# Seven of the sixteen units of a group by 32x32 block transposes and HBM instead of six, in an attention + MoE kernel on Trainium2

## The chip, the cores and the metric

One core of one Trainium2 chip. The time is the device time of one execution in microseconds (us). The kernel before takes 242.75 us (median of 3 runs, 242.49 to 242.84).

## What is computed

Two samples of 512 tokens with 128 channels. The part that fills most of the time, and the only one that the change touches, is attention with a convolution of the scores along the keys:

```python
Q, K, V = (query @ W.T + b, split in 16 heads of 8)
scores  = Q @ K.T / sqrt(8)                     # per head 512 x 512
scores  = conv1d over keys, 3 taps, per head     # H -> H, kernel size 3
weights = softmax(scores)
out     = weights @ V, heads joined, @ Wo.T + bo
```

(The convolution mixes the 16 heads; the kernel folds it into a key tensor of its own for every output head.) Ahead of it stands a gated MLP with one of eight experts for each sample, behind it a low-rank projection and a routed feed-forward layer of eight experts.

## The kernel before, in words

**Units and groups.** Attention is cut into 128 units: 2 samples x 16 heads x 4 tiles of 128 queries. A group is 4 heads, 16 units (u = 0 to 15), and there are 8 groups. A group has two pairs of heads: w = 0 is units 0 to 7, w = 1 is units 8 to 15. For each unit:

- TensorE makes the scores (128 queries x 512 keys) with three matmuls (L855 to L857), four units ahead of the rest, into one of four PSUM banks.
- VectorE takes the row minimum of the negated scores and copies them to SBUF (`maximum`, L592), also four units ahead.
- ScalarE takes the exponential in place (`exp`, L398).
- The weights must be turned so that keys lie on partitions. There are two ways. **By PE**: four transposes on TensorE (L995), and ScalarE copies the PSUM bank to SBUF (L442). **By blocks**: VectorE transposes 32x32 blocks (L719) into a staging tile `TB`, and once for each pair of heads the SP queue writes `TB` to a buffer `swap` in HBM (L218) and reads it back with the blocks in their places into `PTB` (four DMAs, L223).

**Which unit goes which way** is written out by hand: `by_blocks` (L181) takes the units with u % 8 in (0, 3, 5), six of sixteen. The last pair of the last group (`last_pair`) goes by PE alone. `by_pe` and `nth_blocks` number the units of the two ways for the semaphores `eva` (PE ways copied out) and `tb` (block transposes done).

**The crossing.** `cross(pair, w, gi)` (L214) on SP waits for the pair's last block transpose (`tb`), issues the write, waits for its landing (`ts`), issues the four reads (landing counted in `tm`). SP does nothing else in this stretch. For w = 0 the last block transpose is that of unit 5, for w = 1 that of unit 13.

**The outputs.** `outputs(pair, w, gi)` (L861) on TensorE multiplies the turned weights of a pair of heads with the values, once both ways have delivered: it waits for `eva` and for `tm`. It stands at the end of unit 15 for w = 0, and at the end of unit 7 *of the next group* for w = 1. TensorE works strictly in order, so the scores of unit 12 of that next group, issued at its unit 8, stand behind the outputs of w = 1. Four column tiles of 32 (two heads x two halves of each) are used side by side; three of the four have matmuls 256 wide, and the odd head of the half that mixes both ways has twice as many of 128 (L881), since its tiles lie in two buffers, `PTB` and `PTC`. After the outputs of w = 1 VectorE copies the bank out (`raw_out`, L599, at its unit 8) and goes on with its `maximum` of unit 12.

**Order on VectorE.** In unit u: extra work of the unit (`raw_out` at 8, `normalise` at 9, in the second sample parts of the next stages by `AT_DVE`), the maximum of unit u + 4, the block transpose of unit u if it goes by blocks, and at u % 4 = 2 the middle tap of a later head's keys (L536).

Of the kernel before, what the change touches and what calls it, by code (L numbers as in the profile page):

```python
# [19 lines left out]
B, S, C = 2, 512, 128  # L20
# [43 lines left out]
def build(nc, cond, wexp, xT, wqkvo, lora, cols, b2row, w1, w2, consts, out, swap):  # L64
# [4 lines left out]
    with ExitStack() as ctx:  # L69
# [75 lines left out]
        D = sb("D", [128, NT, T], f32r)  # L145

        flat = PT[:, :]
        half, cross_words = 8 * S, 4 * QT * 96
        PTA = flat[:, 0:half].rearrange("p (g k c) -> p g k c", g=G, k=QT)
        PTB = flat[:, half:half + 2 * cross_words].rearrange("p (w i k c) -> p w i k c", w=2, k=QT, i=4)  # L150
        PTC = flat[:, half + 2 * cross_words:16 * S].rearrange("p (w k c) -> p w k c", w=2, k=QT)
        staging = w2s[:, :, :, :].rearrange("p e j c -> p (e j c)")
        TB = staging[:, 0:2 * cross_words].rearrange("p (w i k c) -> p w i k c", w=2, k=QT, i=4)
        PTX = staging[:, cross_words:cross_words + 2048].rearrange("p (h k c) -> p h k c", h=2, k=QT)
        Ub = [[flat[:, (4 * b + i) * 512:(4 * b + i + 1) * 512] for i in range(2)] for b in range(B)]
        Tb = [[flat[:, (4 * b + 2 + i) * 512:(4 * b + 3 + i) * 512] for i in range(2)] for b in range(B)]
        Sb_ = [[flat[:, 4096 + (4 * b + i) * 512:4096 + (4 * b + i + 1) * 512] for i in range(2)] for b in range(B)]
# [21 lines left out]
            return b == B - 1 and isinstance(g, int) and g == NG - 1 and u >= U // 2  # L179

        def by_blocks(b, g, u):  # L181
            return u % 8 in (0, 3, 5) and not last_pair(b, g, u)

        def tile_of(b, g, u):
            return u % QT if last_pair(b, g, u) else TILE[u % 8]
# [1 line left out]
        def by_pe(b, g, u):  # L187


            at = u % 8 // 2 if last_pair(b, g, u) else (None, 0, 1, None, 2, None, 3, 4)[u % 8]  # L190
            return 10 * (NG * b + g) + 5 * (u // 8) + at

        def nth_blocks(b, g, u):
            return 6 * (NG * b + g) + 3 * (u // 8) + (0, 3, 5).index(u % 8)


        @block.sync
        def _(sp):
            sp.dma_start(condS[:, :], cond).then_inc(s["cond"], 16)
            sp.dma_start(xTs[:, 0:S], xT[:, 0:S]).then_inc(s["xt0"], 16)  # L200
            sp.wait_ge(s["cidx"], B)
            for b in range(B):
                e = sp.value_load(cidx[0:1, 8 * b:8 * b + 1], min_val=0, max_val=E - 1)
                for part, at, end in (("up", 0, WGT), ("down", WGT, EW)):
                    sp.dma_start(we[:, b:b + 1, at:end], wexp[bass.ds(e, 1), :, at:end]
                                 .rearrange("e p n -> p e n")).then_inc(s[f"{part}{b}"], 16)
                if b == 0:
                    sp.dma_start(xTs[:, S:T], xT[:, S:T]).then_inc(s["xt1"], 16)
            sp.dma_start(cst[:, :], consts).then_inc(s["cst"], 16)
            sp.dma_start(w1s[:, :, :], w1).then_inc(s["w1"], 16)  # L210
            sp.dma_start(b2s[:, :], b2row).then_inc(s["b2"], 16)
            sp.dma_start(out[T:2 * T, :].rearrange("(p a) c -> p (a c)", p=128), xT).then_inc(s["dump"], 16)

            def cross(pair, w, gi):  # L214

                sp.wait_ge(s["tb"], 3 * pair + 3)
                sp.wait_ge(s["pv"], pair)
                sp.dma_start(swap[:, w, :, :], TB[:, w, :, :, :].rearrange("p i k c -> p i (k c)"))\  # L218
                    .then_inc(s[f"ts{w}"], 16)
                sp.wait_ge(s[f"ts{w}"], 16 * gi + 16)  # L220
                by_source = swap.rearrange("(i p) w j n -> p w j i n", i=4)
                for j in range(4):
                    sp.dma_start(PTB[32 * j:32 * j + 32, w, :, :, :].rearrange("p i k c -> p i (k c)"),  # L223
                                 by_source[:, w, j, :, :]).then_inc(s[f"tm{w}"], 16)

            with sp.Fori(0, B * NG - 1) as g:
                for w in range(2):
                    cross(2 * g + w, w, g)
            cross(2 * (B * NG - 1), 0, B * NG - 1)
            sp.wait_ge(s["pv"], 4 * NG + 2)  # L230
            sp.dma_start(w2s[:, :, :, :], w2).then_inc(s["w2"], 16)
            rows = out[0:T, :].rearrange("(t p) c -> p t c", p=128)
            for b in range(B):
                sp.wait_ge(s["xte"], b + 1)
                sp.dma_start(rows[:, QT * b:QT * (b + 1), :], X1[:, QT * b:QT * (b + 1), :]).then_inc(s["outd"], 16)
            sp.wait_ge(s["outd"], 16 * B)
            sp.wait_ge(s["dump"], 16)
            sp.wait_ge(s["add"], 16 * E)
# [105 lines left out]
        def _(act):  # L344
# [83 lines left out]
            def unit(b, g, u):  # L428

                n = U * (NG * b + g) + u  # L430
                hd = H * b + G * g + u // QT
                if b == 1 and isinstance(g, int) and (g, u) in AT_ACT:
                    after(0, AT_ACT[g, u])
                if u % 2 == 1 if last_pair(b, g, u) else not by_blocks(b, g, u):

                    nth = by_pe(b, g, u)
                    bank = TP[1 if last_pair(b, g, u) else by_pe(0, 0, u) % 2]
                    half_tile, parity = divmod(tile_of(b, g, u), 2)
                    dst = PTA[:, u // QT % G, :, half_tile * 128:(half_tile + 1) * 128] if parity else \
                        PTC[:, u // 8, :, :]  # L440
                    act.wait_ge(s["tp"], nth + 2)
                    act.activation(dst, bank[:, :].rearrange("p (k q) -> p k q", k=QT), ACT.Copy)\  # L442
                        .then_inc(s["eva"], 1)
                if not isinstance(g, int) or n + AHEAD < U * NG * B:
                    exp(n + AHEAD, (u + AHEAD) % RING)
                if u % QT == 3 and (not isinstance(g, int) or hd + 3 < B * H):
                    high_half(hd + 3, (u // QT + 1) % 2)
                if u == 9:
                    stage_values(b, g)
# [51 lines left out]
        def _(dve):  # L501
# [181 lines left out]
            def unit(b, g, u):  # L683
# [22 lines left out]
                if last_pair(b, g, u) and u % 2 == 0:  # L706
                    dve.wait_ge(s["tpx"], (u - U // 2) // 2 + 1)
                    if u == U // 2:
                        dve.wait_ge(s["ts1"], 16 * (B * NG - 1))
                    dve.tensor_copy(PTX[:, j % 2, :, half_tile * 128:(half_tile + 1) * 128],  # L710
                                    TP[0][:, :].rearrange("p (k q) -> p k q", k=QT))\
                        .then_inc(s["evx"], 1)
                elif by_blocks(b, g, u):

                    if u % (2 * QT) == 0 and (not isinstance(g, int) or b + g > 0):
                        dve.wait_ge(s[f"ts{w}"], 16 * (NG * b + g))
                    dve.wait_ge(s["ex"], n + 2)
                    at = 64 * (j % 2) + 32 * half_tile
                    dve.transpose(TB[:, w, :, :, at:at + 32].rearrange("p i k c -> p k i c"),  # L719
                                  Pb[:, u % RING, :].rearrange("p (k i c) -> p k i c", i=4, c=32)).then_inc(s["tb"], 1)  # L720
                if u % QT == 2 and (not isinstance(g, int) or H * b + G * g + j + 3 < B * H):
                    over = isinstance(g, int) and G * g + j + 3 >= H
# [72 lines left out]
        def _(pe):  # L795
# [63 lines left out]
            def outputs(pair, w, gi):  # L859


                pe.wait_ge(s["eva"], 5 * pair + 6)
                pe.wait_ge(s[f"tm{w}"], 64 * gi + 64)
                if w == 0:
                    pe.wait_ge(s["vst"], gi + 1)
# [1 line left out]
                for k in range(QT):  # L867
                    for f in range(2):
                        for i in range(2):
                            at = 32 * (2 * f + i)  # L870
                            bank, v = PV[at:at + VW, 256 * w:256 * w + 256], Vst[:, k, 2 * w + i, :]
                            ends = dict(start=(k == 0), stop=(k == QT - 1))
                            if f:
                                mm = pe.matmul(bank, v, PTA[:, 2 * w + i, k, :], **ends)  # L874
                            elif i == 0:
                                pe.matmul(bank, v, PTB[:, w, :, k, 0:64].rearrange("p i (t c) -> p t i c", t=2), **ends)  # L876
                            else:
                                t = k // 2
                                for kk in (2 * k % QT, 2 * k % QT + 1):
                                    x = PTC[:, w, kk, :] if t else PTB[:, w, :, kk, 64:96]  # L880
                                    pe.matmul(bank[:, 128 * t:128 * t + 128], Vst[:, kk, 2 * w + i, :], x,  # L881
                                              start=(kk == 0), stop=(kk == QT - 1))
                mm.then_inc(s["pv"], 1)

            def last_outputs(l):
# [1 line left out]

                bank = (PV[:, 256:384], SC[3][:, 0:128])[l]
                pe.wait_ge(s["evx"], 3 + l)
                pe.wait_ge(s["eva"], 10 * B * NG - 1 + l)  # L890
                for k in range(QT):
                    for f in range(2):
                        for i in range(2):
# [79 lines left out]
            def unit(b, g, u):  # L973
# [7 lines left out]
                if not by_blocks(b, g, u):  # L981
# [8 lines left out]
                    else:  # L990
                        bank = TP[by_pe(0, 0, u) % 2]
                        if not isinstance(g, int) or nth > 0:
                            pe.wait_ge(s["eva"], nth)
                    for k in range(QT):
                        mm = pe.transpose(bank[:, k * 128:(k + 1) * 128],  # L995
                                          Pb[:, u % RING, k * 128:(k + 1) * 128], ident)
# [178 lines left out]
```

## Time and profile before

| what | value |
|---|---|
| median of 3 runs | 242.75 us |
| the profiled execution | 245.08 us, of which the span is 243.0 us |
| TensorE (PE) busy | 225.3 us, 93% |
| VectorE (DVE) busy | 194.5 us, 80% |
| ScalarE (ACT) busy | 165.1 us, 68% |
| GpSimd (POOL) busy | 162.0 us, 67% |
| chain that ended last | PE 70%, DVE 10%, issue 8%, POOL 4%, ACT 3%, DMA 2% |

Groups run from about 30 us to 200 us of the span. A busy share is an average over stages; a PE that is busy all the time may still run at a lower granted clock (a separate column of the windows view). Start times in the timeline are from the span's start; matmuls overlap one another, so what one costs is the distance from its start to the next one's, not its own duration.

### The profile page before, as it was taken

What the parts mean: (1) busy time and instruction counts of PE and PEld (TensorE: products, weight loads), DVE (VectorE), ACT (ScalarE), POOL (GpSimd) and SP (SyncE); (2) the same over time, 40 slices, a digit from 0 to 9 for tenths busy, and PEclk for the clock granted to TensorE, in tenths of its full rate; (3) what the DMA queues carried; (4) which work ended last, traced back from release to release, by engine and by line L of the source; (5) the groups of instructions that cost most, each with busy time, mean ns of one, the idle gap of its engine ahead of it and who ended that gap; (6) DMA issues with size and microseconds to landing.
All of it is one profiled execution on the core that took longest, in us unless ns stands there. A gap on an engine that the chain in (4) does not pass through costs nothing.

```text
span 243.0 us, 5432 instructions
## 1 busy us (share of the span) xinstructions
PE 225.3 (93%) x1733; PEld 178.3 (73%) x1733; DVE 194.5 (80%) x485; ACT 165.1 (68%) x297; POOL 162.0 (67%) x190
## 2 busy tenths in 40 slices
PE   7897986799989999999999999999999989999980
PEld 7444764588868788878876876878788866688980
DVE  2548899979898998997998899989989783375470
ACT  2554577989788988989778569799798770212510
POOL 1008986889969989898886668889983600052785
PEclk9999799999999999999999999999999999999997
DMA  6990000745627454574535353636476440840233
GB/s 201 364 386 0 0 4 39 205 157 122 207 57 220 166 129 160 121 219 147 132 133 129 132 129 131 132 136 155 154 206 133 161 101 4 294 138 3 22 32 32
DMA packets 14933, 32.77 MB, mean 135 GB/s; under 512 B 1586, under 2 KB 11826, under 8 KB 14642
## 3 DMA queue, kind: packets, MB, share of 16 engines
q1 hardware_dynamic: 13330, 31.35, 42.9%
q0 software_dynamic: 1152, 0.52, 2.5%
q10 hardware_dynamic: 432, 0.65, 0.8%
q8 instruction: 11, 0.18, 0.3%
q14 instruction: 8, 0.07, 0.1%
HBM read 19.67 MB, written 13.37 MB: 136 GB/s over the span
## 4 chain that ended last, share of the span: by engine, by line
PE 70%; DVE 10%; issue 8%; POOL 4%; ACT 3%; DMA 2%; POOLq 1%; SPq 0%; DVEq 0%; ACTq 0%
PE tp L995 12%; PE sc L855 11%; PE sc L857 10%; PE sc L856 10%; PE pvbank L876 6%; PE pvbank L874 5%; POOL out L338 4%; DVE Pb L592 3%; PE sc L1047 2%; PE sc L817 2%; PE sc L1048 1%; DMA we<-in_wexp 1%; PE misc L902 1%; ACT Kh L393 1%; DVE kc L536 1%
## 5 line engine op out<-in xcount | busy, mean ns | idle before, releaser
L398 ACT ACTIVATE Pb<-Pb,nbias 128x512 f32<-128x512 f32 x128 | 90.6, 719 | 26.0 <-DVE Pb L592 24.8
L592 DVE TENSOR_SCALAR_CACHE_REDUCE Pb<-sc,col 128x512 f32<-128x512 f32 x128 | 91.8, 733 | 11.5 <-PE sc L857 10.2
L855 PE MATMUL sc<-Kh,Ql 128*128 128x512 f32 x124 | 57.0, 460 | 3.0 <-POOL Kl L262 1.4
L995 PE MATMUL tp<-cst,Pb 128*128 128x128 f32 x332 | 49.8, 273 | 3.2 <-ACT PT L442 2.3
L995 PEld LDWEIGHTS tp<-cst,Pb 128*128 128x128 f32 x332 | 40.5, 140 | 15.9 <-issue 4.2
L262 POOL TENSOR_TENSOR Kl<-kc,Kh 128x512 fp32r<-128x512 f32 x29 | 37.3, 1287 | 17.9 <-ACT Kh L393 16.7
L857 PE MATMUL sc<-Kh,Qh 128*128 128x512 f32 x124 | 48.9, 394 | 0.0
L856 PE MATMUL sc<-Kl,Qh 128*128 128x512 f32 x124 | 48.7, 393 | 0.0
L442 ACT ACTIVATE PT<-tp 128x512 f32<-128x512 f32 x79 | 45.9, 581 | 1.7 <-PE tp L995 1.2
L274 POOL TENSOR_TENSOR td<-ta,tc_ 128x512 f32<-128x512 f32 x31 | 44.4, 1431 | 2.6
L267 POOL TENSOR_SCALAR ta<-Kp,cwS 128x512 f32<-128x512 f32 x31 | 23.4, 755 | 16.0 <-ACT Kp L371 15.9
L719 DVE STREAM_TRANSPOSE w2s<-Pb 128x512 f32<-128x512 f32 x45 | 31.7, 704 | 0.0
L855 PEld LDWEIGHTS sc<-Kh,Ql 128*128 128x128 f32 x124 | 23.4, 189 | 9.6 <-issue 5.3
L536 DVE SCALAR_TENSOR_TENSOR kc<-Kp,col,td 128x512 f32<-128x512 f32 x31 | 29.5, 952 | 0.0
L874 PE MATMUL pvbank<-PT,Vst 128*32 128x256 f32 x240 | 29.3, 386 | 0.0
L881 PE MATMUL pvbank<-PT,Vst 128*32 128x128 f32 x240 | 29.0, 274 | 0.0
L876 PE MATMUL pvbank<-PT,Vst 128*32 128x256 f32 x120 | 28.7, 382 | 0.2 <-DMA PT<-swap 0.2
L269 POOL TENSOR_SCALAR tc_<-Kp,cwS 128x512 f32<-128x512 f32 x31 | 27.6, 889 | 0.0
L857 PEld LDWEIGHTS sc<-Kh,Qh 128*128 128x128 f32 x124 | 23.3, 188 | 5.5
L881 PEld LDWEIGHTS pvbank<-PT,Vst 128*32 128x32 f32 x240 | 25.0, 110 | 0.0
L856 PEld LDWEIGHTS sc<-Kl,Qh 128*128 128x128 f32 x124 | 23.6, 190 | 1.8 <-issue 0.2
L393 ACT ACTIVATE Kh<-kc 128x512 fp32r<-128x512 f32 x30 | 18.5, 617 | 0.9 <-DVE kc L536 0.9
(213 smaller groups left out, 289.4 us busy)
## 6 DMA issues: line engine op xcount, KB each, us to landing
swap<-w2s SPq DMA_DIRECT2D x15, 768.0 KB, 3.3
PT<-swap SPq DMA_DIRECT2D x60, 192.0 KB, 3.9
w1s<-in_w SPq DMA_DIRECT2D x1, 2048.0 KB, 9.7
w2s<-in_w SPq DMA_DIRECT2D x1, 2048.0 KB, 10.1
cst<-in_consts SPq DMA_DIRECT2D x1, 652.0 KB, 5.2
xTs<-in_xT SPq DMA_DIRECT2D x2, 256.0 KB, 3.3
we<-in_wexp SPq DMA_DIRECT2D x2, 256.0 KB, 3.6
b2s<-in_b2row SPq DMA_DIRECT2D x1, 512.0 KB, 10.4
```

Of the source, the lines that this page charges most:

```text
L262: pool.tensor_tensor(Kl[:, n, :], kc[:, n, :], Kh[:, n, :].bitcast(f32), ALU.subtract)\
L274: pool.tensor_tensor(td[:, n, :], ta[:, :], tc_[:, :], ALU.add).then_inc(s["d"], 1)
L398: act.activation(Pb[:, k, :], Pb[:, k, :], ACT.Exp, bias=nbias[:, k:k + 1], scale=-1.0)\
L442: act.activation(dst, bank[:, :].rearrange("p (k q) -> p k q", k=QT), ACT.Copy)\
L592: dve.tensor_scalar(Pb[:, k, :], SC[k % 4][:, :], cb, None, ALU.subtract, ALU.min, accum_out=nbias[:, k:k + 1]).then_inc(s["mx"], 1)
L855: pe.matmul(SC[k][:, :], ql, Kh[:, h2, :], start=True, stop=False)
L856: pe.matmul(SC[k][:, :], qh, Kl[:, h2, :], start=False, stop=False)
L857: pe.matmul(SC[k][:, :], qh, Kh[:, h2, :], start=False, stop=True).then_inc(s["sc"], 1)
L874: mm = pe.matmul(bank, v, PTA[:, 2 * w + i, k, :], **ends)
L876: pe.matmul(bank, v, PTB[:, w, :, k, 0:64].rearrange("p i (t c) -> p t i c", t=2), **ends)
L881: pe.matmul(bank[:, 128 * t:128 * t + 128], Vst[:, kk, 2 * w + i, :], x, start=(kk == 0), stop=(kk == QT - 1))
L995: mm = pe.transpose(bank[:, k * 128:(k + 1) * 128], Pb[:, u % RING, k * 128:(k + 1) * 128], ident)
```

## The change

`by_blocks` takes unit 15 too, so that seven units of a group go by blocks: units 0, 3, 5 for w = 0 and units 8, 11, 13, 15 for w = 1. Nine go by PE instead of ten. The numbers in the semaphore waits follow. `cross` for w = 1 waits for the transpose of unit 15 instead of unit 13, and moves four words of width 32 for every block column instead of three: 512 words for each row piece instead of 384. `swap` becomes one tensor with rows of 896 words, of which w = 0 has the first 384 and w = 1 the other 512, so a partition's four pieces no longer lie behind one another in HBM. In `outputs` the odd head of w = 1 now lies wholly in `PTB`, so its matmuls are 256 wide; the one of w = 0 stays as it was. TensorE's wait at unit 1 is for one more `eva`, since nine is odd and units 14 and 1 now use the same PSUM bank. Nothing changes in the last pair of the last group.

```diff
@@ -145,13 +145,15 @@
-        half, cross_words = 8 * S, 4 * QT * 96
+        half, cross_words = 8 * S, (4 * QT * 96, 4 * QT * 128)
...
@@ -179,7 +181,7 @@
         def by_blocks(b, g, u):
-            return u % 8 in (0, 3, 5) and not last_pair(b, g, u)
+            return (u % 8 in (0, 3, 5) or u == U - 1) and not last_pair(b, g, u)
@@ -188,10 +190,10 @@
-            return 10 * (NG * b + g) + 5 * (u // 8) + at
+            return 9 * (NG * b + g) + 5 * (u // 8) + at
 
         def nth_blocks(b, g, u):
-            return 6 * (NG * b + g) + 3 * (u // 8) + (0, 3, 5).index(u % 8)
+            return 7 * (NG * b + g) + 3 * (u // 8) + (0, 3, 5, 7).index(u % 8)
@@ -213,15 +215,15 @@
             def cross(pair, w, gi):
 
-                sp.wait_ge(s["tb"], 3 * pair + 3)
+                sp.wait_ge(s["tb"], 3 * pair + gi + (3 + w))
                 sp.wait_ge(s["pv"], pair)
-                sp.dma_start(swap[:, w, :, :], TB[:, w, :, :, :].rearrange("p i k c -> p i (k c)"))\
-                    .then_inc(s[f"ts{w}"], 16)
+                crossing = swap[:, :, 384 * w:384 + 512 * w]
+                sp.dma_start(crossing, TB[w].rearrange("p i k c -> p i (k c)")).then_inc(s[f"ts{w}"], 16)
                 sp.wait_ge(s[f"ts{w}"], 16 * gi + 16)
-                by_source = swap.rearrange("(i p) w j n -> p w j i n", i=4)
+                by_source = crossing.rearrange("(i p) j n -> p j i n", i=4)
                 for j in range(4):
-                    sp.dma_start(PTB[32 * j:32 * j + 32, w, :, :, :].rearrange("p i k c -> p i (k c)"),
-                                 by_source[:, w, j, :, :]).then_inc(s[f"tm{w}"], 16)
+                    sp.dma_start(PTB[w][32 * j:32 * j + 32, :, :, :].rearrange("p i k c -> p i (k c)"),
+                                 by_source[:, j, :, :]).then_inc(s[f"tm{w}"], 16)
@@ -861,7 +861,7 @@
             def outputs(pair, w, gi):
 
-                pe.wait_ge(s["eva"], 5 * pair + 6)
+                pe.wait_ge(s["eva"], 9 * gi + (6, 10)[w])
                 pe.wait_ge(s[f"tm{w}"], 64 * gi + 64)
@@ -873,11 +875,14 @@
+                            elif w:
+                                mm = pe.matmul(bank, v, PTB[w][:, :, k, 64:128].rearrange("p i (t c) -> p t i c", t=2),
+                                               **ends)
                             else:
                                 t = k // 2
                                 for kk in (2 * k % QT, 2 * k % QT + 1):
-                                    x = PTC[:, w, kk, :] if t else PTB[:, w, :, kk, 64:96]
+                                    x = PTC[:, kk, :] if t else PTB[w][:, :, kk, 64:96]
@@ -990,7 +995,7 @@
-                            pe.wait_ge(s["eva"], nth)
+                            pe.wait_ge(s["eva"], nth + 1 if u == 1 else nth)
@@ -1168,7 +1173,7 @@
-    swap = nc.dram_tensor("swap", (128, 2, 4, 384), mybir.dt.float32, kind="Internal").ap()
+    swap = nc.dram_tensor("swap", (128, 4, 896), mybir.dt.float32, kind="Internal").ap()
```

## Rows read from the trace of the kernel before

**Rows 1.** Costliest groups (busy, mean ns, idle before and its releaser): the outputs
```profile
L876 PE MATMUL pvbank<-PT,Vst 128*32 128x256 f32 x120 | 28.7, 382 | 0.2 <-DMA PT<-swap 0.2
```

**Rows 2.** Windows: us, busy of PE, PEld, DVE, ACT, POOL, PEclk, DMA
```profile
83.65:94.11 10.46, 10.46 (x92) 8.49 (x89) 9.99 (x27) 9.09 (x16) 9.22 (x11) 1.00 0.51 143
94.11:103.97 9.86, 9.86 (x88) 8.12 (x85) 8.84 (x22) 8.62 (x16) 8.86 (x10) 1.00 0.54 150
```

**Rows 3.** Timeline of PE: start, duration, line, operation; outputs, then units
```profile
102.03 0.40 PE L876 MATMUL pvbank<-PT,Vst 128*32 128x256 f32 x1
...
106.03 0.60 PE L995 MATMUL tp<-cst,Pb 128*128 128x128 f32 x4
...
107.16 0.60 PE L995 MATMUL tp<-cst,Pb 128*128 128x128 f32 x4
...
108.30 0.39 PE L855 MATMUL sc<-Kh,Ql 128*128 128x512 f32 x1
...
108.99 0.60 PE L995 MATMUL tp<-cst,Pb 128*128 128x128 f32 x4
```

**Rows 4.** Timeline of DVE at the end of a group (units 13 to 16)
```profile
91.42 0.70 DVE L719 STREAM_TRANSPOSE w2s<-Pb 128x512 f32<-128x512 f32 x1
92.05 0.70 DVE L592 TENSOR_SCALAR_CACHE_REDUCE Pb<-sc,col 128x512 f32<-128x512 f32 x1
...
93.41 0.74 DVE L592 TENSOR_SCALAR_CACHE_REDUCE Pb<-sc,col 128x512 f32<-128x512 f32 x1
...
95.18 0.75 DVE L592 TENSOR_SCALAR_CACHE_REDUCE Pb<-sc,col 128x512 f32<-128x512 f32 x1 [1.02 <-PE sc L857]
```

**Rows 5.** Timeline of SP, third group, w = 1: write and four reads issued
```profile
92.15 0.34 SPq L218 DMA_DIRECT2D swap<-w2s  x1
95.41 1.73 SPq L223 DMA_DIRECT2D PT<-swap  x4
```

**Rows 6.** DMA view of single issues: slowest write; first and last reads of a crossing
```profile
swap<-w2s SPq DMA_DIRECT2D x1, 768.0 KB, 5.4
...
PT<-swap SPq DMA_DIRECT2D x1, 192.0 KB, 2.9
...
PT<-swap SPq DMA_DIRECT2D x1, 192.0 KB, 4.3
```

**Rows 7.** Chain that ended last: the load of 16 numbers (64 bytes)
```profile
0.73 1.20 DMA condS<-in_cond
```

**Rows 8.** Timeline of SP: w = 1 writes of groups 0, 3 and 4
```profile
49.77 0.34 SPq L218 DMA_DIRECT2D swap<-w2s  x1
...
112.21 0.34 SPq L218 DMA_DIRECT2D swap<-w2s  x1
...
135.64 0.34 SPq L218 DMA_DIRECT2D swap<-w2s  x1
```

**Rows 9.** Timeline of PE: the outputs that those writes lead to
```profile
60.42 0.40 PE L876 MATMUL pvbank<-PT,Vst 128*32 128x256 f32 x1
...
123.25 0.40 PE L876 MATMUL pvbank<-PT,Vst 128*32 128x256 f32 x1
...
148.51 0.40 PE L876 MATMUL pvbank<-PT,Vst 128*32 128x256 f32 x1
```

**Rows 10.** Timeline of DVE in group 4: maxima of units 18 and 20
```profile
135.53 0.71 DVE L592 TENSOR_SCALAR_CACHE_REDUCE Pb<-sc,col 128x512 f32<-128x512 f32 x1
...
140.56 0.75 DVE L592 TENSOR_SCALAR_CACHE_REDUCE Pb<-sc,col 128x512 f32<-128x512 f32 x1
```

**Rows 11.** Windows ahead of the first groups (columns as in rows 2)
```profile
22.50:24.70 2.20, 0.02 (x2) 0.05 (x1) 2.11 (x4) 1.20 (x2) 2.10 (x3) 1.00 0.00 0
...
25.00:26.00 1.00, 1.00 (x5) 0.77 (x3) 1.00 (x2) 0.33 (x1) 0.92 (x2) 0.65 0.00 0
26.00:28.00 2.00, 2.00 (x6) 1.63 (x5) 1.66 (x5) 1.13 (x3) 1.86 (x3) 0.50 0.00 0
28.00:29.00 1.00, 1.00 (x4) 0.77 (x4) 0.62 (x1) 0.61 (x1) 1.00 (x2) 0.65 0.00 0
```

More of the change, by code:

```diff
@@ L147, in build @@
         flat = PT[:, :]
-        half, cross_words = 8 * S, 4 * QT * 96
+        half, cross_words = 8 * S, (4 * QT * 96, 4 * QT * 128)
         PTA = flat[:, 0:half].rearrange("p (g k c) -> p g k c", g=G, k=QT)
-        PTB = flat[:, half:half + 2 * cross_words].rearrange("p (w i k c) -> p w i k c", w=2, k=QT, i=4)
-        PTC = flat[:, half + 2 * cross_words:16 * S].rearrange("p (w k c) -> p w k c", w=2, k=QT)
+        PTB = [a.rearrange("p (i k c) -> p i k c", k=QT, i=4) for a in
+               (flat[:, half:half + cross_words[0]], flat[:, half + cross_words[0]:half + sum(cross_words)])]
+        PTC = flat[:, half + sum(cross_words):16 * S].rearrange("p (k c) -> p k c", k=QT)
         staging = w2s[:, :, :, :].rearrange("p e j c -> p (e j c)")
-        TB = staging[:, 0:2 * cross_words].rearrange("p (w i k c) -> p w i k c", w=2, k=QT, i=4)
-        PTX = staging[:, cross_words:cross_words + 2048].rearrange("p (h k c) -> p h k c", h=2, k=QT)
+        TB = [a.rearrange("p (i k c) -> p i k c", k=QT, i=4) for a in
+              (staging[:, 0:cross_words[0]], staging[:, cross_words[0]:sum(cross_words)])]
+        PTX = staging[:, cross_words[0]:sum(cross_words)].rearrange("p (h k c) -> p h k c", h=2, k=QT)
         Ub = [[flat[:, (4 * b + i) * 512:(4 * b + i + 1) * 512] for i in range(2)] for b in range(B)]
@@ L439, in unit @@
                     dst = PTA[:, u // QT % G, :, half_tile * 128:(half_tile + 1) * 128] if parity else \
-                        PTC[:, u // 8, :, :]
+                        PTC[:, :, :]
                     act.wait_ge(s["tp"], nth + 2)
@@ L718, in unit @@
                     at = 64 * (j % 2) + 32 * half_tile
-                    dve.transpose(TB[:, w, :, :, at:at + 32].rearrange("p i k c -> p k i c"),
+                    dve.transpose(TB[w][:, :, :, at:at + 32].rearrange("p i k c -> p k i c"),
                                   Pb[:, u % RING, :].rearrange("p (k i c) -> p k i c", i=4, c=32)).then_inc(s["tb"], 1)
@@ L875, in outputs @@
                             elif i == 0:
-                                pe.matmul(bank, v, PTB[:, w, :, k, 0:64].rearrange("p i (t c) -> p t i c", t=2), **ends)
+                                pe.matmul(bank, v, PTB[w][:, :, k, 0:64].rearrange("p i (t c) -> p t i c", t=2), **ends)
+                            elif w:
+                                mm = pe.matmul(bank, v, PTB[w][:, :, k, 64:128].rearrange("p i (t c) -> p t i c", t=2),
+                                               **ends)
                             else:
@@ L889, in last_outputs @@
                 pe.wait_ge(s["evx"], 3 + l)
-                pe.wait_ge(s["eva"], 10 * B * NG - 1 + l)
+                pe.wait_ge(s["eva"], 9 * B * NG + l)
                 for k in range(QT):
```

## The prediction

> **What bounds the kernel now.** First the windows, to see which engine has no gap. In a settled group of 20.32 us PE is busy in all of it at the full granted clock, 10.46 us for the half with units 8 to 15 and 9.86 us for the other; DVE is busy for 9.99 and 8.84 us, ACT for less, POOL for 9.22 and 8.86 us [rows 2]. So a settled group costs what PE's queue costs, and DVE has 1.5 us to spare in it. Then the costliest groups, for what PE waits for ahead of the outputs: DMA made it wait 0.2 us in the whole execution [rows 1]. The crossings through HBM are hidden. The question that these two views leave open is by how much, since the change makes a crossing both later and larger; the timelines of SP and PE answer it.
>
> **What it removes.** From transpose to transpose a unit that goes by PE takes 107.16 - 106.03 = 1.13 us of PE, a unit by blocks 108.99 - 108.30 = 0.69 us [rows 3], so unit 15 frees 0.44 us. It does so in seven groups (not in the last): 3.1 us, which is the whole gain if nothing else moves. The odd head's matmuls go from eight of 128 columns to four of 256. The columns are the same, and the other three column tiles stream 256 of them at the same time, so I take nothing for it; between 0 and 0.1 us a group of issuing may go. ACT has one copy less in each, and it is not the bound.
>
> **What it adds on DVE.** A block transpose takes 92.05 - 91.42 = 0.63 us. It stands behind the maximum of unit 19. There DVE ran out of work: that maximum starts at 93.41, would be done by 94.15, and the next starts at 95.18 after 1.02 us of waiting for scores [rows 4]. The transpose fits in this gap even when PE comes 0.44 us sooner. If the cover were gone it would cost 0.63 us a group. TensorE's changed wait at unit 1 is for a copy made two units earlier; nothing for it. On SP the next crossing (w = 0) waits for a transpose of unit 5, some 7 us later, while issuing the larger one holds SP 4.0 + 1.8 us, so SP is free again; that write may queue behind the reads of the larger crossing, but its own outputs are then later too.
>
> **What it moves: the start of the crossing of w = 1.** Before, the write is issued at 92.15, right behind the transpose of unit 13 (91.42 + 0.63) [rows 4, 5]. Now the wait is for unit 15's. Between the two DVE has the maximum of 18, a middle tap, the maximum of 19 (93.41 - 92.05 = 1.36 us to its start, 0.67 us for itself by the same spacing as its neighbours) and the transpose, 0.63 us: **2.65 us later**.
>
> **And its length.** Before, the write of 768 KB lands in 95.41 - 92.15 = 3.26 us [rows 5]. Now it is 1 MB. The nearest rows bound what the third more costs: nothing, if the time is not in the bytes (3.3 us), or in proportion (4.35 us). With 1.2 us of it fixed, as in the load of 64 bytes [rows 7], it is 1.2 + 2.06 x 4/3 = **4.0 us**, which I take; the writes have also taken up to 5.4 us [rows 6]. Of the four reads, issued over 1.73 us (0.43 apart), the first lands after 2.9 us and the fourth 1.30 + 4.3 = 5.6 us after the first issue [rows 5, 6], so three more reads of 192 KB cost 2.7 us, 0.9 us each, twice their issue spacing: they queue for bandwidth. With 256 KB I take 1.2 us each and 3.2 us for the first, **6.8 us**; the ends are 5.6 us (the count of pieces sets the time, and it is the same) and 7.5 us (all in proportion). With 0.06 us between landing and first read [rows 5] and 0.1 us for PE to start, a crossing from the end of the transpose to the outputs is 0.1 + 4.0 + 0.06 + 6.8 + 0.1 = 11.1 us.
>
> The Trainium skill, "DMA: Bandwidth & Descriptors" (section on the two cost components), gives a DMA about 2.0 us fixed and 436 GB/s beyond. By it the write of 1 MB would take 4.4 us, 0.4 us more than taken above, but 3.8 us for the old one, where the trace has 3.26; the measurement decides.
>
> **How much room there was.** From the issue of the write to the outputs: third group 102.03 - 92.15 = 9.88 us [rows 3, 5], and groups 1, 5 and 6 lie within 0.25 us of it (four in all, taken at 9.85); group 0 60.42 - 49.77 = 10.65; group 3 123.25 - 112.21 = 11.04; group 4 148.51 - 135.64 = 12.87 [rows 8, 9]. New need, counted from the old issue: 2.65 + 4.0 + 0.06 + 6.8 + 0.1 = 13.61 us. In group 4 DVE has the gate work between the two transposes: from 135.53 to 140.56 and a transpose of 0.63 [rows 10], 5.66 us in place of 2.65, so 16.6 us. PE then stands still at the end of unit 7 for longer than before: 3.0 us (group 0), 4 x 3.76 = 15.0, 2.6 (group 3), 3.75 (group 4): **24.4 us**. Is any of it got back? Behind the outputs PE has scores 12, and DVE its copy of the bank and every maximum up to 19, then the next trigger; that way from outputs to trigger was DVE's without a gap already, so the lost time is lost in every turn. And PE's 0.44 us is not on this loop at all: it only makes PE wait earlier. So the 3.1 us are **not** subtracted.
>
> **The clock.** PE stood still from 22.5 to 24.7 us ahead of the first groups, and the granted clock then fell from full (2.4 GHz) to half (1.2 GHz) over about 3.4 us: 0.65, 0.50, 0.50, 0.65 in the microseconds from 25 to 29 [rows 11]. The new stalls, the wait above plus the freed 0.44 us, are of 3 to 4.2 us, longer than that one. If each is followed by such a stretch, up to 1.7 us of PE's work is lost in it, and part of the stretch lies in the stall itself. Between 0 and 1.7 us I take 0.9 us, seven times: **6.3 us**.
>
> The Trainium skill, "TensorE: Matmul & The Clock Gate" (section "HAM oscillation"), describes the same: PE waiting for a DMA in each turn goes back to half rate each time. The row agrees so far that one idle stretch did it; no row shows whether it repeats.
>
> **Sum.** Against the profiled execution: 245.08 + 24.4 + 6.3 = 275.8 us. That execution is 2.3 us above the median of the runs, 242.75; the added terms are the same for both, so I predict **273.5 us** for the median.
>
> **Rivals.**
> - *Stalls without the clock.* PE does 20 us of work between stalls, and small gaps elsewhere left the clock full [rows 2]. For it: only one stretch in the trace shows a fall. Then 242.75 + 24.4 = 267.2 us, between 261 and 273 with the bounds on the transfers.
> - *Size costs nothing*, only the later start does (3.3 and 5.6 us). Each stall is 1.9 us shorter: 24.4 - 13.3 = 11.1, 253.9 us. Against it: the reads queue at 0.9 us each. Stalls of under 2 us would hardly touch the clock.
> - *The other side, faster.* The crossing stays hidden, and PE's 0.44 us count: 242.75 - 3.1 = 239.65 us. It decides at a crossing of 9.88 - 2.65 - 0.44 = 6.8 us from trigger to outputs; the present one, smaller, already takes 3.26 + 5.6 = 8.9 us. I see nothing in the trace that would shorten it.
> - *The change does nothing measurable*, because gains and stalls cancel (0.44 us a stall). Every settled group would have to stall that little.
>
> **Chances.** Stalls and half clock 0.50 (own range 265 to 284); stalls, full clock 0.33; size free 0.12; faster 0.03; no difference 0.02. A difference of 0.2%, about what a measurement of this kernel can tell, is 0.5 us, and no case but the last lies in it. The range goes from 256 (between size-free and full clock) to 283 (half clock with slower transfers: the writes at 4.35, the reads at 7.5 us would add 1.05 x 7 = 7.4 us).
>
> **What would show it.** PE idle ahead of the first outputs matmul of w = 1 (L876), released by the DMA into PT, about 3 to 4 us long and seven times; the write of w = 1 issued right behind the transpose of unit 15, landing in 4.0 us; the last read 6.8 us after the first issue; the group's period near 24 us in place of 20.3; DVE and ACT with idle time in the same place; seven dips in the granted clock right behind the stalls. It is wrong if L876's idle is under 10 us in sum, if the write is issued sooner than 2 us behind unit 13's transpose, or if the clock stays full.

## The result, and the profile after

The changed kernel takes **285.25 us** (median of 4 runs, 284.34 to 288.94) against 242.8 us: a ratio of 1.171, with a 95% interval of 1.165 to 1.177. It is 42.5 us slower, 2.3 us above the upper end of the range and 11.8 us above the forecast of 273.5 us. The execution whose trace is shown took 288.94 us, with a span of 286.9 us and a mean granted clock of 0.906; the other three took 284.3 to 286.1 us at 0.920 to 0.923, and the ratio is that of these three fast runs alone, which is why it lies below 285.25 / 242.8 = 1.175.

The page of the profile, busy time, granted clock in 40 slices, and the chain that ended last:

```profile
PE 239.8 (84%) x1649; PEld 178.5 (62%) x1649; DVE 197.8 (69%) x492; ACT 161.8 (56%) x290; POOL 159.0 (55%) x190
...
PEclk9997999986997799689959997899699959999998
...
PE 36%; DMA 26%; DVE 19%; issue 9%; SPq 3%; POOL 3%; ACT 1%; POOLq 1%; DVEq 0%
DMA PT<-swap 14%; DMA swap<-w2s 11%; DVE Pb L594 9%; PE pvbank L878 8%; PE sc L857 4%; DVE w2s L721 4%; POOL out L340 3%; PE tp L1000 3%; PE sc L859 3%; PE sc L858 3%; SPq L225 3%; DVE kc L538 2%; PE sc L1052 1%; PE sc L819 1%; PE sc L1053 1%
```

PE has fallen from 93% to 84% of a longer span, and DMA has gone from 2% to 26% of the chain. Each crossing of w = 1 stands in it now, both its halves.

The costliest groups, with the idle time before them and what ended it. What was 0.2 us in [rows 1] is now 29.9 us (28.8 us of it ahead of the seven outputs of w = 1, 1.0 us ahead of the first outputs of w = 0), and the copy behind the outputs (L601) waits as well:

```profile
L878 PE MATMUL pvbank<-PT,Vst 128*32 128x256 f32 x120 | 40.4, 498 | 29.9 <-DMA PT<-swap 29.9
L601 DVE COPY RAW<-pvbank 128x512 f32<-128x512 f32 x7 | 4.8, 692 | 41.9 <-PE pvbank L876 41.9
```

Timeline of PE, one turn of the loop: outputs of w = 1 and the scores behind them, then the next outputs of w = 1:

```profile
91.49 0.60 PE L878 MATMUL pvbank<-PT,Vst 128*32 128x256 f32 x1 [4.62 <-DMA PT<-swap]
...
95.06 0.80 PE L857 MATMUL sc<-Kh,Ql 128*128 128x512 f32 x1
...
118.76 0.61 PE L878 MATMUL pvbank<-PT,Vst 128*32 128x256 f32 x1 [4.87 <-DMA PT<-swap]
```

A period, from one set of outputs of w = 1 to the next, is 27.3 us instead of 20.3. The outputs take 3.57 us from their start to the next scores, where they took 83.61 - 81.71 = 1.90 us, though the odd head's are fewer. The kernel before, PE and then DVE (the maximum of unit 12), in the same turn:

```profile
81.71 0.40 PE L876 MATMUL pvbank<-PT,Vst 128*32 128x256 f32 x1
...
83.61 0.50 PE L855 MATMUL sc<-Kh,Ql 128*128 128x512 f32 x1
...
84.76 0.75 DVE L592 TENSOR_SCALAR_CACHE_REDUCE Pb<-sc,col 128x512 f32<-128x512 f32 x1 [0.32 <-PE sc L857]
```

The seven stalls on the DMA are 3.34, 4.62, 4.87, 3.69, 2.96, 4.78 and 4.58 us long.

Timeline of DVE in the same turn, the copy of the bank, the maximum of unit 12, then the maximum of unit 19, the transpose of unit 15, and the first step of the next group:

```profile
95.19 0.69 DVE L601 COPY RAW<-pvbank 128x512 f32<-128x512 f32 x1 [6.15 <-PE pvbank L876]
96.89 0.75 DVE L594 TENSOR_SCALAR_CACHE_REDUCE Pb<-sc,col 128x512 f32<-128x512 f32 x1 [1.01 <-PE sc L859]
...
105.66 0.74 DVE L594 TENSOR_SCALAR_CACHE_REDUCE Pb<-sc,col 128x512 f32<-128x512 f32 x1
...
106.33 0.70 DVE L721 STREAM_TRANSPOSE w2s<-Pb 128x512 f32<-128x512 f32 x1
106.96 0.70 DVE L594 TENSOR_SCALAR_CACHE_REDUCE Pb<-sc,col 128x512 f32<-128x512 f32 x1
```

Timeline of SP: the crossing of w = 1 that this transpose releases, then that of w = 0:

```profile
107.06 0.52 SPq L221 DMA_DIRECT2D swap<-w2s  x1
111.47 1.73 SPq L225 DMA_DIRECT2D PT<-swap  x4
113.76 0.52 SPq L221 DMA_DIRECT2D swap<-w2s  x1
120.28 1.73 SPq L225 DMA_DIRECT2D PT<-swap  x4
```

The write goes out 0.10 us behind unit 15's transpose (106.33 + 0.63, the spacing to the next step) and lands in 4.4 us; from the first read to the outputs it is 118.76 - 111.47 = 7.29 us. The fourth read is issued at 112.77 and takes 5.9 us:

```profile
PT<-swap SPq DMA_DIRECT2D x1, 256.0 KB, 5.9
```

It lands at 118.67, and PE starts 0.1 us behind it. That makes 11.7 us from the write's issue to the outputs (11.5 to 11.7 us in all seven). The write of w = 0 queues behind the reads and takes 6.5 us in place of 3.3, but nobody waits for it: behind the first, no outputs of w = 0 stand still.

The windows of the stall, of the outputs, of the stretch to the maximum of unit 12 and of the rest (columns as in [rows 2]):

```profile
86.90:91.40 4.50, 0.00 (x0) 0.00 (x0) 2.14 (x5) 3.06 (x6) 4.15 (x6) 0.83 1.05 244
91.40:95.10 3.70, 3.61 (x33) 1.63 (x33) 0.00 (x0) 0.00 (x0) 3.38 (x5) 0.50 0.49 165
95.10:97.00 1.90, 1.90 (x11) 1.52 (x8) 0.80 (x2) 0.00 (x0) 0.00 (x0) 0.58 0.97 222
97.00:107.00 10.00, 10.00 (x85) 8.18 (x84) 9.73 (x26) 7.92 (x14) 3.68 (x4) 1.00 0.05 10
```

The clock falls from 2.4 to 1.2 GHz inside the stall already (0.83 is a third of it at half), stays there through the outputs, and comes back just before the maximum of unit 12: 1.5 + 3.7 + 1.6 = 6.8 us at half rate, twice the fall in [rows 11]. From the start of the outputs to the maximum of unit 12 it is 96.89 - 91.49 = 5.40 us; before, with a full clock, 84.76 - 81.71 = 3.05 us. Behind that point DVE sets the pace, almost without a gap, as before: 107.06 - 96.89 = 10.17 us to the write.

### The profile page after: what moved, and what is told of

Read it like the earlier page. It is cut to its first block, busy times and chain, and to the rows that moved or that the text cites. A ratio compares the mean times of both kernels' runs of the same rounds, so it can differ in the third digit from the quotient of the medians.

```text
span 286.9 us, 5254 instructions
## 1 busy us (share of the span) xinstructions
PE 239.8 (84%) x1649; PEld 178.5 (62%) x1649; DVE 197.8 (69%) x492; ACT 161.8 (56%) x290; POOL 159.0 (55%) x190
## 4 chain that ended last, share of the span: by engine, by line
PE 36%; DMA 26%; DVE 19%; issue 9%; SPq 3%; POOL 3%; ACT 1%; POOLq 1%; DVEq 0%
DMA PT<-swap 14%; DMA swap<-w2s 11%; DVE Pb L594 9%; PE pvbank L878 8%; PE sc L857 4%; DVE w2s L721 4%; POOL out L340 3%; PE tp L1000 3%; PE sc L859 3%; PE sc L858 3%; SPq L225 3%; DVE kc L538 2%; PE sc L1052 1%; PE sc L819 1%; PE sc L1053 1%
## 5 line engine op out<-in xcount | busy, mean ns | idle before, releaser
L594 DVE TENSOR_SCALAR_CACHE_REDUCE Pb<-sc,col 128x512 f32<-128x512 f32 x128 | 91.8, 732 | 11.7 <-PE sc L859 10.4
L878 PE MATMUL pvbank<-PT,Vst 128*32 128x256 f32 x120 | 40.4, 498 | 29.9 <-DMA PT<-swap 29.9
L857 PE MATMUL sc<-Kh,Ql 128*128 128x512 f32 x124 | 59.5, 480 | 4.1 <-DVE Pb L594 1.6
L858 PE MATMUL sc<-Kl,Qh 128*128 128x512 f32 x124 | 50.4, 407 | 0.0
L1000 PE MATMUL tp<-cst,Pb 128*128 128x128 f32 x304 | 45.8, 274 | 2.3 <-ACT PT L444 1.8
L1000 PEld LDWEIGHTS tp<-cst,Pb 128*128 128x128 f32 x304 | 37.5, 141 | 13.8 <-issue 4.1
L444 ACT ACTIVATE PT<-tp 128x512 f32<-128x512 f32 x72 | 41.9, 582 | 1.7 <-PE tp L1000 1.6
L276 POOL TENSOR_TENSOR td<-ta,tc_ 128x512 f32<-128x512 f32 x31 | 41.3, 1333 | 2.6
L878 PEld LDWEIGHTS pvbank<-PT,Vst 128*32 128x32 f32 x120 | 15.1, 136 | 42.6 <-issue 39.4
L876 PE MATMUL pvbank<-PT,Vst 128*32 128x256 f32 x240 | 41.0, 501 | 0.0
L721 DVE STREAM_TRANSPOSE w2s<-Pb 128x512 f32<-128x512 f32 x52 | 36.6, 704 | 0.0
L857 PEld LDWEIGHTS sc<-Kh,Ql 128*128 128x128 f32 x124 | 24.2, 195 | 16.3 <-issue 10.4
L601 DVE COPY RAW<-pvbank 128x512 f32<-128x512 f32 x7 | 4.8, 692 | 41.9 <-PE pvbank L876 41.9
L880 PE MATMUL pvbank<-PT,Vst 128*32 128x256 f32 x56 | 25.3, 634 | 0.0
```

Source lines behind the costliest of these rows:

```text
L276: pool.tensor_tensor(td[:, n, :], ta[:, :], tc_[:, :], ALU.add).then_inc(s["d"], 1)
L594: dve.tensor_scalar(Pb[:, k, :], SC[k % 4][:, :], cb, None, ALU.subtract, ALU.min, accum_out=nbias[:, k:k + 1]).then_inc(s["mx"], 1)
L721: dve.transpose(TB[w][:, :, :, at:at + 32].rearrange("p i k c -> p k i c"), Pb[:, u % RING, :].rearrange("p (k i c) -> p k i c", i=4, c=32 ...
L857: pe.matmul(SC[k][:, :], ql, Kh[:, h2, :], start=True, stop=False)
L858: pe.matmul(SC[k][:, :], qh, Kl[:, h2, :], start=False, stop=False)
L878: pe.matmul(bank, v, PTB[w][:, :, k, 0:64].rearrange("p i (t c) -> p t i c", t=2), **ends)
```

## The experiments

The theory that these results suggest: the crossing's start is on a loop (outputs, VectorE's half group, crossing, outputs); its length is mis-sized by 0.6 us a turn, and each stall costs another 2.4 us through the clock (5.40 - 3.05 us).

**e1_fill: the changed kernel with PE kept busy in the stall.**

```diff
                 pe.wait_ge(s["eva"], 9 * gi + (6, 10)[w])
+                if w:
+                    keep_busy(PV[:, 256:384], 16)
                 pe.wait_ge(s[f"tm{w}"], 64 * gi + 64)
```

> The changed kernel with sixteen 128-column matmuls of ones ahead of TensorE's wait for the w = 1 crossing, into the half of the output bank that the real ones overwrite: about 16 x 0.22 = 3.5 us of work that lies inside the stall of some 4.6 us. Theory (stall, and a clock that falls behind each): the granted clock stays full, the outputs take 1.9 us again instead of 3.6, the way from outputs to the maximum of unit 12 is 3.0 us instead of 5.4; seven times 2.4 us are gained, 285.25 - 16.8 = 268.5 us. Rival (the excess over the prediction is in the transfers, the clock is a bystander because VectorE sets the pace behind the outputs): no gain, 285 us, or slower where the extra matmuls reach beyond a stall.

Measured 273.4 us (1.123, 1.115 to 1.132): matmuls that compute nothing make the kernel 11.8 us *faster*. The windows of the fill and of the outputs, the wait that is left, and the next write of w = 1:

```profile
84.90:88.50 3.60, 3.60 (x33) 3.46 (x31) 2.26 (x5) 3.17 (x6) 3.42 (x4) 1.00 1.05 213
89.30:91.20 1.90, 1.89 (x33) 0.97 (x33) 0.00 (x0) 0.00 (x0) 1.90 (x3) 1.00 0.58 219
```
```profile
89.31 0.40 PE L880 MATMUL pvbank<-PT,Vst 128*32 128x256 f32 x1 [0.76 <-DMA PT<-swap]
```

```profile
102.50 0.52 SPq L221 DMA_DIRECT2D swap<-w2s  x1
```

The clock is full and the outputs take 1.86 us in all seven turns. From the outputs to the next write it is 13.2 us (89.31 to 102.50) in place of 15.6 us (91.49 to 107.06): the clock's price is **2.4 us a turn**, and the same difference in the five other turns is 2.3 to 2.4 us. Between the two traces it is 14.8 us (spans of 286.9 and 272.1 us), where 7 x 2.4 us would be 16.8. Of the difference 1.6 us is the way from the write to the outputs: here it was 0.2 to 0.6 us longer in five turns and 0.3 to 0.4 us shorter in two. In groups 0 and 4 that is in part the fill itself, which ends 0.3 and 0.5 us behind the landing of the last read; for the rest I have no cause.

Between the medians only 11.8 of the expected 16.8 us came. The other three executions of the changed kernel spent less time at half clock: by their mean granted clock and span, an estimate of 43.5 to 45.2 us each, where the traced one has 53.9 us. So the clock's price in them is smaller, 11.8 us or, with the 1.6 us of the crossings added, 13.4 us: an estimate of 1.7 to 1.9 us a turn.

**e2_later: the kernel before, the crossing started later and nothing else.**

```diff
                 sp.wait_ge(s["tb"], 3 * pair + 3)
+                if w:
+                    sp.wait_ge(s["mx"], 8 * pair + 13)
                 sp.wait_ge(s["pv"], pair)
```

> The kernel before, with one edit: the crossing of w = 1 also waits for VectorE's maximum of unit 19, 2.0 us behind the transpose of unit 13. No work is added or left out. Theory (the crossing's start sits on the path as soon as the room is used up): need 2.0 + 0.1 + 3.3 + 5.9 = 11.3 us against 9.85 us of room in groups 1, 2, 5 and 6 (1.45 us each), 10.65 (0.65), 11.04 (0.3) and some 12.9 in group 4, where the start moves by 5 us (1.4): about 8 us in sum, 251 us; the clock stays full at stalls this short, or falls once or twice at 2.4 us each. Rival (the room is larger than read, TensorE's own queue sets the time): 243 us.

Measured 252.1 us (1.037, 1.031 to 1.044). Two microseconds of delay in a transfer that was hidden cost 9.3 us (about 8 us were expected). The outputs start up to 1.8 us later than in an undelayed turn, all take 1.90 us but one (2.05), and the clock stays full (0.994 over the span). So the room was as small as read, and in this trace waits of up to 1.7 us left the clock alone.

**e3_unit13 and e4_small: either half of the mis-fit alone.** In e3 the crossing has its new size and its new layout in HBM, but the block units are 8, 11, 12 and 13, so that it starts behind unit 13:

```diff
-TILE = (0, 1, 3, 2, 1, 0, 3, 2)
+TILE = (0, 1, 3, 2, 1, 0, 3, 2, 0, 1, 3, 2, 2, 0, 3, 1)
+BLOCKS = (0, 3, 5, 8, 11, 12, 13)
...
-            return (u % 8 in (0, 3, 5) or u == U - 1) and not last_pair(b, g, u)
+            return u in BLOCKS and not last_pair(b, g, u)
...
```

> The changed kernel with the four block units of the second half at 8, 11, 12 and 13 instead of 8, 11, 13 and 15 (query tiles of the last head reordered), so that the crossing has the new size but starts behind unit 13 again. Theory: from the transpose of 13 the crossing needs 0.1 + 4.4 + 7.2 = 11.7 us, and the extra transpose ahead of it 0.6; against 9.95 us of room a stall of 2.35 us, in sum about 14.6 us. With a full clock 257.4 us; if seven stalls of that length still bring the clock down at 2.4 us each, 274 us. Rival (only the later start counts, size is free): 243 us or less.

In e4 the start is that of the change, but unit 15's blocks go to words of their own and are left out of the outputs, and 768 KB cross, in rows laid out as in the kernel before:

```diff
-        half, cross_words = 8 * S, (4 * QT * 96, 4 * QT * 128)
+        half, cross_words = 8 * S, (4 * QT * 96, 4 * QT * 96)
...
+                    turned_blocks = UNMOVED if u == U - 1 else TB[w][:, :, :, at:at + 32]
...
```

> The changed kernel with the crossing at its old size of 768 KB: unit 15 is turned in blocks and awaited, but its blocks are not moved, and the output matmuls read other columns in their place (the attention of these tiles is left wrong). Theory: the start is 2.65 us later as before, the crossing takes 3.3 + 6.0 us; a stall of 2.05 us in a usual group, 12.5 us in sum: 255.3 us at a full clock, 272 us if every stall brings the clock down. Rival (start is harmless, size is what costs): 243 us.

Measured: e3 261.5 us (1.076, 1.069 to 1.083), e4 256.8 us (1.054, 1.046 to 1.063). Neither half alone is harmless, and both together cost more than their sum (18.7 + 14.0 against 42.5 us). A small part of that is in the stalls, 14.0 and 11.6 us in sum against 28.8 us, since each half alone may use up the same spare room; the larger part is in the clock, which stands at half for 20.5 and 3.4 us behind the stalls against 47.8 us in the trace of the change. e3's 261.5 us lie between its two forecasts, 257.4 us at a full clock and 274 us with seven falls. e4's clock-free estimate of 255.3 us was close; the one set of outputs at reduced clock took 2.71 us, behind a stall of 2.29 us:

```profile
106.70 0.38 PE L880 MATMUL pvbank<-PT,Vst 128*32 128x256 f32 x1 [2.29 <-DMA PT<-swap]
```

while one of 2.26 us, of group 5, left it full. In e3 five of the seven outputs took 2.9 to 3.6 us, behind stalls of 2.2 to 3.3 us; the one behind 1.51 us took 1.86 us:

```profile
86.48 0.38 PE L880 MATMUL pvbank<-PT,Vst 128*32 128x256 f32 x1 [2.27 <-DMA PT<-swap]
...
89.34 0.80 PE L859 MATMUL sc<-Kh,Ql 128*128 128x512 f32 x1
...
134.73 0.38 PE L880 MATMUL pvbank<-PT,Vst 128*32 128x256 f32 x1 [1.51 <-DMA PT<-swap]
...
136.59 0.50 PE L859 MATMUL sc<-Kh,Ql 128*128 128x512 f32 x1
```

**e5_hidden: the work of the change with the crossing hidden.** As e4, and the crossing starts behind unit 13 again:

```diff
-                sp.wait_ge(s["tb"], 3 * pair + gi + (3 + w))
+                sp.wait_ge(s["tb"], 3 * pair + gi + 3)
```

> As the last one, but the crossing of w = 1 starts behind unit 13 as in the kernel before, so that unit 15's block transpose is done and never awaited. What is left of the change is the work alone: four transposes and a copy less, a block transpose more, four output matmuls 256 wide instead of eight of 128. Theory (TensorE bounds a settled group, the crossing stays hidden): 242.75 - 3.1 = 239.7 us. Rival (VectorE, with 0.63 us more a group, takes over): 242.5 to 244 us. Since the room shrinks by 0.44 us, stalls of some tenths may take part of the gain in groups 1, 5 and 6.

Measured 243.7 us (1.002, 0.997 to 1.007), as the rival said and not 239.7 us. The 3.1 us are not there even when nobody waits for the crossing. To find who takes them, two more:

**e6_none**: e5 without unit 15's block transpose on VectorE (a small memset signals in its place, and unit 15's part of the result is left out), and **e7_extra**: the kernel before with that transpose added where the change has it.

```diff
+                    if u == U - 1:
+                        dve.memset(spare[:, 2:3], 0.0).then_inc(s["tb"], 1)
+                        return
```
```diff
+                if u == U - 1 and not last_pair(b, g, u):
+                    dve.wait_ge(s["ex"], n + 2)
+                    dve.transpose(staging[:, 3584:4096].rearrange("p (k i c) -> p k i c", i=4, c=32),
+                                  Pb[:, u % RING, :].rearrange("p (k i c) -> p k i c", i=4, c=32))\
+                        .then_inc(s["turned"], 1)
...
```

> As e5_hidden, and unit 15's block transpose on VectorE is left out as well (a memset of one column signals in its place), so that unit 15 is turned by nobody and its part of the attention is wrong. Against e5_hidden this takes away 0.6 us of VectorE in seven groups. Theory now (work alone gained only 0.2 us because VectorE pays where it has no gap: the way into group 1 and group 4 with the gate work): about 241 us, 2 us under e5_hidden. Rival (VectorE's part was free and the 3.1 us were never to be had on TensorE): no different from e5_hidden.

> The kernel before with a block transpose of unit 15 added on VectorE at the place where the change has it, into words that nobody reads; TensorE, ScalarE and the crossings as before. Theory: hidden in settled groups (a gap of 1.02 us stands there), 0.6 us each in group 0 or 1 and in group 4: 244 us. Rival (VectorE bounds every group): 242.8 + 7 x 0.63 = 247.2 us. Or nothing at all: 242.8 us.

Measured: e6 0.993 (0.989 to 0.998) of before, which is some 241 us as expected; but the medians of all executions are 242.7 and 242.8 us, so that this gain is at the edge of what can be told. e7 245.0 us, 1.007 (1.003 to 1.011), near the expected 244 us. The windows from one set of w = 1 outputs to the next, for groups 2 and 4, in the kernel before:

```profile
81.71:102.03 20.32, 20.32 (x174) 16.61 (x173) 18.83 (x46) 17.57 (x32) 18.07 (x21) 1.00 0.54 155
123.25:148.51 25.26, 24.48 (x193) 19.05 (x192) 22.79 (x61) 18.42 (x33) 16.62 (x19) 1.00 0.44 125
```

in e5_hidden:

```profile
79.28:99.26 19.98, 19.90 (x161) 15.35 (x160) 19.55 (x48) 17.44 (x31) 18.34 (x21) 1.00 0.56 157
120.05:146.32 26.27, 24.50 (x182) 17.71 (x181) 23.13 (x60) 18.14 (x32) 16.67 (x19) 1.00 0.40 115
```

in e6_none:

```profile
79.38:99.33 19.95, 19.95 (x162) 15.36 (x161) 18.48 (x46) 16.76 (x30) 18.31 (x21) 1.00 0.55 158
120.08:145.14 25.06, 24.02 (x182) 17.83 (x181) 21.99 (x60) 17.95 (x32) 16.93 (x19) 1.00 0.42 120
```

and in e7_extra:

```profile
81.40:102.72 21.32, 20.53 (x174) 16.61 (x173) 20.53 (x48) 17.98 (x32) 18.20 (x21) 1.00 0.53 148
123.88:150.44 26.56, 25.00 (x193) 18.94 (x193) 24.21 (x62) 18.70 (x34) 16.45 (x19) 1.00 0.43 119
```

The first number after the window is the period. A settled group does give 0.34 to 0.37 us when PE has less to do. Group 4, where the gate of the first sample runs on VectorE, gives 0.20 us without the transpose (25.06) and costs 1.01 us with it (26.27): a swing of 1.2 us for one instruction of 0.63 us. Over the six periods between the outputs of w = 1, e5 is 0.2 us shorter than before and e6 0.7 us; in e6 PE waited once more for the crossing, 0.69 us in group 5. e7 costs 1.00 us in group 2 and 1.30 us in group 4 and next to nothing in the other four, so my expectation of where it costs was wrong: group 2 is one of the settled ones.

**e9_contig: the change with HBM regions in one piece.**

```diff
-                crossing = swap[:, :, 384 * w:384 + 512 * w]
+                crossing = swap[:, 1536 * w:1536 + 2048 * w].rearrange("p (j n) -> p j n", j=4)
```

> The changed kernel with the buffer in HBM laid out so that each pair of heads has a region of its own, a partition's four pieces one behind another (6 and 8 KB) as in the kernel before, instead of pieces of 1.5 and 2 KB at a stride of 3.5 KB. Sizes, starts and work are those of the change. The write of 1 MB took 4.4 us in the changed kernel, where 4.0 was predicted from the bytes. Theory (the excess is in the shorter pieces): 4.0 us, and since the write lies in the loop that sets the time, 7 x 0.4 = 2.9 us are gained, 282.4 us. Rival (the bytes cost more than read): 4.4 us and 285.2 us.

Measured 277.9 us (1.145, 1.133 to 1.157), 7.3 us below the change. The DMA issues of the changed kernel, and of e9 (KB each, median us to landing):

```profile
swap<-w2s SPq DMA_DIRECT2D x7, 1024.0 KB, 4.4
PT<-swap SPq DMA_DIRECT2D x28, 256.0 KB, 4.8
swap<-w2s SPq DMA_DIRECT2D x8, 768.0 KB, 6.4
```
```profile
swap<-w2s SPq DMA_DIRECT2D x7, 1024.0 KB, 3.9
PT<-swap SPq DMA_DIRECT2D x28, 256.0 KB, 4.6
```

The half microsecond of the write is in the pieces, as the theory said, and the way from the write to the outputs is 0.6 us shorter (11.0 against 11.6 us on average), 4.3 us in seven turns. But 2.9 us were expected and 7.3 came. The rest goes with the clock: it stands at half for 27.3 us behind the stalls where the trace of the change has 47.8 us, and only in the last three turns did the outputs take 3.5 to 3.6 us, in the other four 1.9 to 3.2 us. Why it fell for less is open. The stalls are shorter (2.8 to 4.2 us), but their length alone does not tell: behind one of 3.96 us the clock was at half for 3.4 us, behind one of 3.34 us in the change for 6.8 us, and behind one of 2.97 us it stayed full.

**e10_all**: e3 with e9's layout and nine filling matmuls.

> The best of seven block units that these parts give: block units 8, 11, 12, 13 (start behind unit 13), the region in HBM in one piece, and nine 128-column matmuls of ones (2.0 us) in the stalls of some 2 to 2.8 us. Theory: e3_unit13 (261.5 us) less 7 x 0.4 us of write and less its five falls of the clock at 1 to 2.4 us each (some 7 us): about 252 us, and still above the kernel before by the stalls that are left, 7 x 1.3 us. Rival (the crossing is hidden by now): 243 us or less.

Measured 256.3 us (1.053, 1.042 to 1.064), 4 us above the expected 252 us. The clock is full in every turn (all outputs 1.86 us), here in the windows of a stall with its fill and of the outputs behind it:

```profile
80.94:83.40 2.46, 2.46 (x23) 2.42 (x21) 2.11 (x5) 2.10 (x5) 2.46 (x3) 1.00 1.00 332
83.48:85.34 1.86, 1.86 (x33) 0.94 (x32) 0.00 (x0) 0.85 (x2) 1.59 (x3) 1.00 0.12 50
```

It is still 13.5 us slower, because the outputs of w = 1 start some 2.5 us behind unit 7's transposes instead of 0.5 us. Part of that is the fill and not the crossing. In group 2 the last read is issued at 99.78 and has landed at 105.18, and PE is still in its fill:

```profile
PT<-swap SPq DMA_DIRECT2D x1, 256.0 KB, 5.4
```
```profile
103.85 2.17 PE L803 MATMUL pvbank<-ones 128*128 128x128 f32 x18
105.95 0.40 PE L882 MATMUL pvbank<-PT,Vst 128*32 128x256 f32 x1
```

In groups 1 to 5 the outputs start 0.4, 0.8, 1.1, 2.3 and 0.5 us behind the landing, where 0.1 us is usual. The 4.5 us in sum beyond that are about what the kernel lies above its forecast; I put them down to the fill (an estimate: no run has a shorter one). So e10_all isn't the best that these parts give. Yet e5_hidden gains nothing even with the crossing hidden, so I expect no arrangement of seven units that only hides the crossing to beat the kernel before; that is argued, not shown.

**e8_warm: the kernel before with nine filling matmuls ahead of the first scores**, where its profile has the fall of [rows 11].

> The kernel before with nine 128-column matmuls of ones (2 us) in TensorE's idle stretch ahead of the first scores, where the granted clock falls to half for 3.4 us in the profile of before. Nothing else is changed. If the idle stretch is the cause, the clock stays full there and up to 1.4 us are gained, 241.4 to 242.8 us; the kernel e5_hidden and e3_unit13 had no fall there in their profiled executions, so before may miss it in some of its own runs too, and the median may move less.

Measured 243.4 us (1.000, 0.997 to 1.004), no difference. In its profile the clock is full in that stretch, but it is so in that of e5_hidden too, which has no filling there:

```profile
22.00:30.00 8.00, 5.16 (x26) 4.01 (x25) 7.88 (x15) 4.96 (x8) 7.61 (x9) 1.00 0.00 0
```

The same idle stretch brings the clock down in one execution and not in another. The spread differs: of the 29 executions of the kernel before, eight took 244.5 to 245.4 us and one 247.3 us, while all twelve with the filling took 242.4 to 243.9 us. Whether the filling does that is not shown.

## Why the prediction was right, and where it was wrong

**Right: the mechanism and its sign.** The write is issued 2.65 us later, right behind unit 15's transpose; the crossing takes more than the room; PE stands still seven times; the 0.44 us are not on the loop; DVE behind the outputs has no gap and gives nothing back; the clock falls behind each stall of the traced execution. e2_later shows the first alone, e4 and e3 the two halves.

**Wrong: the term for the clock.** "Between 0 and 1.7 us I take 0.9 us": in the traced execution it measured 2.4 us a turn (e1_fill), beyond the upper bound, and in the others an estimate of 1.7 to 1.9 us, at the bound or just above it. The bound took over the 3.4 us at half rate from the one fall in the trace of before. Here each of the seven lasted 6.8 us, of which about 5.3 us lay on PE's work, and everything up to the maximum of unit 12 was on the loop. That is 7 x (2.4 - 0.9) = 10.4 us in the trace, and 5.5 to 7.1 us by the medians.

**Wrong: the length of the crossing.** Predicted 11.0 us from the issue of the write to the outputs, measured 11.6 us, so 7 x 0.6 = 4.2 us more. The write was sized by its bytes as 4.0 us, and by bytes it is 3.9 us (e9_contig); but the change also cuts each partition's contiguous row into four pieces at a stride, 4.4 us. The diff showed this, and the prediction costed only the size. The fit that the prediction quotes from the Trainium skill, "DMA: Bandwidth & Descriptors" (section "Anatomy of one DMA"), stands there for DMAs that GpSimd issues, and these are SP's. That it gives 4.4 us for the write is no confirmation: laid out in one piece, the write took 3.9 us. The reads were short by the rest: the fourth lands 1.3 + 5.6 to 5.9 = 6.9 to 7.2 us behind the first issue, not 6.8, and PE starts 0.1 us behind it, as predicted. (The 0.06 us that the prediction puts between landing and first read stands in none of its rows; it weighs nothing here.)

**Wrong: the upper end of the range.** The clock's term alone brings the forecast of 273.5 us to 279.0 to 280.6 us by the medians, still inside; with the crossing's 4.2 us it is outside. But the range didn't carry the prediction's own bounds. 283 us is 275.8 us, the sum for the slower profiled execution, plus 7.4 us for slower transfers; from the forecast for the median that makes 280.9 us. The clock's bound was left out of it: 7 x (1.7 - 0.9) = 5.6 us more gives 286.5 us, and the measured 285.25 us lies below that.

Together: 24.4 + 4.2 + 7 x 2.4 = 45.4 us against 43.9 us between the two spans. The sum is 1.5 us too high, and the runs don't say in which term. Of the medians, 24.4 + 4.2 + 13.4 = 42.0 us against 42.5 us, with the clock's part estimated as above.

**Wrong, without weight here: the gain of 3.1 us and the transpose at nothing.** The rival "faster" named a crossing short enough to win, and e5_hidden is in that case, since PE nowhere waits for the crossing, and doesn't win. PE's gain shows in settled groups (0.34 us in group 2) and not in group 1, or in group 4 with the transpose. VectorE's transpose has a gap to hide in on average, not in every group: added alone it costs 2.2 us by the medians, 1.7 us by the ratio (e7_extra).

## What to carry to other kernels

A transfer whose trigger is moved is to be measured against its room, from the issue to the first use, not against the engines' busy shares; here 10 us of room held a 9 us crossing, and every microsecond beyond came back seven times. Where PE stalls in a loop, the price is the stall plus what the lowered clock makes of the work behind it; a few matmuls into a dead half of a bank show in one run which is which, as long as they are shorter than the stall; in e10_all they were longer than it and cost time of their own. A layout that packs two regions of different width into common rows changes the pieces of a DMA too, and wants a price of its own.

## What the runs showed of the hardware that I had not expected

Half clock for 6.8 us behind stalls of 3 to 5 us, again in each turn of the traced execution, where the only fall before lasted 3.4 us; behind stalls of 2.8 to 4.2 us in e9_contig it was 6.8 us twice, 3.4 us four times and nothing once. Waits of up to 1.7 us left it full (e2_later), and of two of 2.3 us in e4_small one brought it down and one did not. The same 1 MB to HBM took 3.9 us in pieces of 8 KB and 4.4 us in pieces of 2 KB, and the instruction that issues it held SP's queue for 0.34 us (e9_contig) and 0.52 us (the change). A write queued behind the reads of another crossing on the same queue landed after 6.5 us instead of 3.3 us.
